# A queue order in a two-layer kernel: ScalarE takes one group's transposed input out of PSUM ahead of the other group's second square

## The reference

```
h = layernorm(x) * (1 + ca) + sa ;  x = x + ga * attention(h)
h = layernorm(x) * (1 + cb) + sb ;  x = x + gb * ffn(h)

fp4_linear(x, w) = fp4_quant_dequant(x) @ fp4_quant_dequant(w).T     # blocks of 16
ffn(h) = fp4_linear(silu(fp4_linear(h, w_gate)) * fp4_linear(h, w_up), w_down)   # 128 -> 352 -> 128
```

## Time and profile before

| | us |
|---|---|
| median of 3 runs | 1372.24 |
| lowest, highest | 1369.85, 1372.98 |
| the profiled execution's own time | 1373.02 |
| its span in the profile | 1371.2 |
| busy in the span: PE, DVE, POOL, ACT | 1128.8, 1057.5, 930.0, 625.6 |
| TensorE's mean granted clock | 0.899 of full speed |

### The profile page before, as it was taken

How to read it: one execution, slowest core, us unless ns; L and a number is a source line. 1 busy time by engine, 2 the same in 40 slices (tenths; PEclk the granted TensorE clock), 3 DMA queues, 4 the chain that set the end, 5 groups by cost and what they waited for, 6 DMA issues and landing times. The chain is left out here.

```text
span 1371.2 us, 29825 instructions
## 1 busy us (share of the span) xinstructions
PE 1128.8 (82%) x10832; PEld 711.5 (52%) x10832; DVE 1057.5 (77%) x1468; ACT 625.6 (46%) x1217; POOL 930.0 (68%) x808
## 2 busy tenths in 40 slices
PE   5889999989999989999999996586657776856865
PEld 2245565645655645655655655354335554545654
DVE  4588968868878768779789776677797777789895
ACT  2245645536546446455456452345444343423332
POOL 3379878768788768798798773333578686684331
PEclk9699999999999989999999997688868886887988
DMA  5112112112111111121121120000000000000000
GB/s 151 35 36 59 37 32 60 41 27 56 41 44 41 37 40 47 36 54 43 28 56 43 31 57 21 8 1 1 0 0 0 1 1 1 0 8 9 9 16 23
DMA packets 48627, 42.17 MB, mean 31 GB/s; under 512 B 7869, under 2 KB 46808, under 8 KB 48472
## 3 DMA queue, kind: packets, MB, share of 16 engines
q1 hardware_dynamic: 48040, 39.36, 11.6%
q10 hardware_dynamic: 432, 0.79, 0.2%
HBM read 6.42 MB, written 2.10 MB: 6 GB/s over the span
## 5 line engine op out<-in xcount | busy, mean ns | idle before, releaser
L509 ACT ACTIVATE a_probs<-a_ps_s 128x512 f32<-128x512 f32 x512 | 303.8, 596 | 326.6 <-PE a_ps_s L417 322.4
L742 POOL TENSOR_TENSOR a_p_lo<-a_probs 128x512 f16<-128x512 f32 x384 | 419.0, 1113 | 34.2 <-ACT a_probs L509 31.8
L670 DVE TENSOR_REDUCE a_nmx<-a_ps_m 128x2 f32<-128x1024 f32 x256 | 311.4, 1217 | 34.6 <-PE a_ps_m L400 33.9
L433 PE MATMUL a_ps_o<-a_v_hi,a_probs 128*128 128x65 f16 x2048 | 244.1, 196 | 15.4 <-DVE a_p_lo L677 7.9
L434 PE MATMUL a_ps_o<-a_v_lo,a_probs 128*128 128x64 f16 x2048 | 241.4, 194 | 0.0
L435 PE MATMUL a_ps_o<-a_v_hi,a_p_lo 128*128 128x65 f16 x2048 | 241.1, 195 | 0.0
L433 PEld LDWEIGHTS a_ps_o<-a_v_hi,a_probs 128*128 128x128 bf16 x2048 | 189.9, 99 | 87.9 <-issue 58.9
L415 PE MATMUL a_ps_s<-a_qq,a_kk 128*128 128x512 f16 x512 | 198.0, 387 | 8.2 <-issue 5.3
L434 PEld LDWEIGHTS a_ps_o<-a_v_lo,a_probs 128*128 128x128 bf16 x2048 | 191.8, 99 | 25.1 <-issue 1.5
L417 PE MATMUL a_ps_s<-a_qq,a_k_l 65*128 65x512 f16 x512 | 198.3, 387 | 0.0
L435 PEld LDWEIGHTS a_ps_o<-a_v_hi,a_p_lo 128*128 128x128 f16 x2048 | 191.5, 98 | 0.0
(11 more groups left out here) (234 smaller groups left out, 2108.7 us busy)
## 6 DMA issues: line engine op xcount, KB each, us to landing
a_qq<-a_rhi SPq DMA_DIRECT2D x128, 128.0 KB, 2.4
a_qq<-a_rlo SPq DMA_DIRECT2D x128, 64.0 KB, 2.1
a_kk<-a_rhi SPq DMA_DIRECT2D x64, 64.0 KB, 2.0
a_k_l<-a_rlo SPq DMA_DIRECT2D x32, 64.0 KB, 2.1
out_x<-x_sb SPq DMA_DIRECT2D x8, 256.0 KB, 2.3
a_qq<-a_nmT SPq DMA_DIRECT2D x64, 2.0 KB
a_probs<-in_wq ACTq DMA_DIRECT2D x1, 512.0 KB, 5.1
a_wo<-in_wo SPq DMA_DIRECT2D x1, 512.0 KB, 12.3
```

The costliest lines, as they stand in the source:

```text
L433: nc.tensor.matmul(out, hi, v_hi[:, b % 2, kt, g, 0:65], start=(kt == 0), stop=False)
L509: nc.scalar.activation(probs[:, p % 2, kt, h, :], ps_s[:, i % 2, :], ACT.Exp, scale=DH0 ** -0.5).then_inc(exp_done, 1)
L670: nc.vector.tensor_reduce(nmx[:, p % 2, i:2 * QT:QT], ps_m[:, n % 2, :, :], axis=X, op=ALU.max, negate=True).then_inc(free[n % 2], 1)
L742: nc.gpsimd.tensor_tensor(p_lo[:, p % 2, kt, h, :], pr, pr.bitcast(BF16)[:, 1:2 * L:2], ALU.subtract).then_inc(lo_pool, 1)
```

## The change

T1 moves from the third `place_group` call to the second, where it stands between S2 and C2. In the shared ticks, the list before reads C2, KVG (or LY, PS), T1; the list after reads T1, C2, KVG (or LY, PS). The order changes for ScalarE and TensorE. In the ticks with KVG, T1 also has an earlier place in the ring, so the KVG of the tick change banks. No instruction, size or wait is added or taken away.

```diff
     each(place_group, ("GH0", "HS", "GU1", "GH1", "C1", "N1"))
     each(place_round, ("SM", "SR", "RES", "ON", "DEN"))
-    each(place_group, ("S2", "C2"))
+    each(place_group, ("S2", "T1", "C2"))
     each(place_round, ("LHT", "KVG", "OT", "LY", "PS", "LX"))
-    each(place_group, ("TD", "T1"))
+    each(place_group, ("TD",))
     each(place_round, ("PP", "SP", "GATE", "SIG"))
```

## The result

The changed kernel takes 1377.71 us (median of 18 executions, 1374.0 to 1386.46) against 1371.09 for the kernel before (18 executions, 1369.02 to 1375.45): a ratio of 1.0055 with a 95% interval of [1.004, 1.0071], so it is slower by 7.5 us (0.0055 of 1371; the interval is 5.5 to 9.7; the two medians are 6.6 us apart). The forecast was 1370.8 us with a range up to 1375.4.

A forecast was written before the change was run, and what follows sets the result against it. It took the second part to be bound by a chain passing from engine to engine, DVE not full. Its per-group terms summed to 1.4 us gained from the 1372.24 us median: 1370.8 us, range 1366.8 to 1375.4.

The forecast's parts named there:

- rival C: The change doesn't do what it says: GU has no slack to give, signs cancel; 0, time 1372.2 us; chance 0.13.
- T1 of 1: Group 1's T1: GU starts earlier, but HS ends with GpSimd's product; +0.5 us gained, bounds 0 and 2.3.
- Groups 8, 10 and 12: T1's transposes move into TensorE's pause before LY, shortening the path by their own slot; +1.65 us gained in sum.
- T1 of 4: Group 4's T1 trades places with KVG on TensorE, so GU starts after four KVG; -0.3 us, a loss.
- 13: Group 13's T1: C2 about 1 us later but just hidden, GU 0.9 earlier, HS ends with GpSimd's product; 0.
- 7: Group 7's T1: GpSimd is the bound, its product starts without idle time; 0.
- T1 of 6: Group 6's T1 trades places with KVG on a cold clock, GU comes later; -0.9 us, bounds 0 and -2.4.
- Rival A: Two-input instructions' windows decide: HS gets in before GpSimd's next product; gain 4 us, time 1368.2; chance 0.25.
- T1 of 14 and 15: Last ticks: T1's copy is late, so C2 comes 0.69 us later and DVE's N2 with it; -0.7 and -1.3 us.
- rival B: Slower: ScalarE's queue holds the square behind a copy that isn't ready; +3.2 us, time 1375.4; chance 0.17.
- T1 of 9: Group 9's T1: its transposes no longer stand between C2 and the following KVG; +0.9 us gained, bounds 0 and 1.1.
- T1 of 2 and 3: TensorE's bank wait goes for group 2 (+0.85 us); DVE's waits for two Silu go for group 3 (+0.7 net).

The follow-up runs named there:

- e2: T1 moved ahead of C2 only for groups 4, 6 and 9, all else the kernel before: 1378.68 us, ratio 1.0042.
- x1: The changed kernel, but in groups 13 to 15 ScalarE does C2 before T1's copy, as in the kernel before: 1374.49 us, ratio 1.002.
- e1: T1 moved ahead of C2 only for groups 13, 14 and 15, all else the kernel before: 1379.29 us, ratio 1.0044.
- w6: The changed kernel plus extra identity products in the tail, none ahead of GU: 1377.37 us, ratio 1.003 against the kernel before.
- a1: The changed kernel plus one extra DVE memset at the start of the second part: 1377.76 us, ratio 1.0038 against the kernel before.
- a2: The changed kernel plus three extra DVE memsets at the start of the second part: 1385.45 us, ratio 1.0092 against the kernel before.
- w3: The kernel before with T1 early for groups 13 to 15 and extra identity products, none ahead of GU: 1373.76 us, ratio 1.001.
- e6: For groups 13 to 15 T1 placed behind C2, which gives the kernel before's instruction lists, so a repeat of it: 1373.87 us, ratio 1.0006.
- w1: The kernel before plus extra identity products from group 12 on, also ahead of GU: 1378.85 us, ratio 1.0041.
- w5: Extra identity products, none ahead of GU, T1 of groups 13 to 15 behind C2; otherwise the kernel before: 1376.27 us, ratio 1.0026.
- c1: The kernel before plus one DVE memset of 0.48 us at the start of the second part: 1376.18 us, ratio 1.0019.
- w4: The kernel before plus extra identity products in the tail, none ahead of GU: 1377.71 us, ratio 1.0033.

## Why the prediction was wrong

What was right. The change does what it says (rival C falls). T1 of 1 brings 0.64 (forecast 0.5; its own two times, 891.9 and 892.56, differ by 0.66), for the reason given: HS now runs beside GpSimd's product and ends with it. By the rule of the Trainium skill that the prediction cited (page "SBUF — State Buffer", section "Who interferes with whom") the two exclude each other, and the trace agrees once more: 2.63 us beside it, 0.83 clear of it. Groups 8, 10 and 12 bring 0.6, 0.7 and 0.4, together 1.7 (forecast 1.65). T1 of 4 costs 0.6 (forecast 0.3), of 13 nothing in itself; 7 brings 0.6 where I had 0. T1 of 6 costs 1.0 in the trace of the change (forecast 0.9), but 3.7 in that of e2 with the same order there, so this agreement is luck. Rival A's first window opened: HS at 1224.59, which the prediction calls group 12's and which is group 11's, takes 1.14 us instead of the 2.50 of the earlier trace rows. DVE keeps this only until 1232, where L1324, which also reads two SBUF tensors, takes 2.31 us beside GpSimd's product instead of 0.69; none of A's 2.6 us came.

The steps that failed:

- **T1 of 14 and 15: -0.7 and -1.3.** This was the mechanism of rival B, which got only 0.17. The queue's own cost was right: 2.0 forecast, 2.2 measured as waits of DVE for C2. Its size on the path was not: 5.5 us in the trace, 5.4 against x1's and 4.8 in time. The term was mis-sized because it priced only the wait. Of TensorE's work behind the waits, the down products twice and the second half of GU met a lower clock, and that costs 3.2 us more. My upper bound of 2.8, two whole squares, was no bound, since it had no term for the products behind them.
- **T1 of 9: +0.9.** It is -1.0 to -1.3. The KVG products and the PS behind them took the durations of the low clock throughout (the last two KVG 2.14 each and PS 3.66, where before the last KVG's large product took 1.52 and PS 2.05), and DVE's wait for Silu rose from 1.80 to 3.09 us at 1180. The order was as foreseen, and the durations were carried over from a trace in which the clock had risen at 1176.6 us instead of 1178.3, 3.4 us earlier as counted from the start of the second part. In e2's trace, where PS ran at the high clock, the same order gained 0.5.
- **T1 of 2 and 3: +0.85 and +0.7.** Both are about 0. In the tick of 2, TensorE's wait of 0.85 did go and GU starts 0.7 us earlier, but DVE's lead behind it is 0.7 us as well: the 0.64 that group 1 had gained, and no second gain. DVE, which had come to N2 earlier by those 0.64, spends them on a longer wait for C2 (2.34 us instead of 1.51). The prediction added the two gains. In the tick of 3 the wait for C2 rises by 1.3 (1.52 to 2.81), against 1.2 that the waits for Silu give back; GU there starts 1.3 us earlier and then runs at the low clock (4.87 us for eight products).

The sum of these: tail 3.5, T1 of 9 2.0, T1 of 2 and 3 1.5, together 7.0, against the 6.9 between a forecast gain of 1.4 and a traced loss of 5.5. What the first two have in common is that durations from the trace before were moved along with their products, as if TensorE's clock moved along too. One reading of the prediction doesn't matter for its sum: it says that the copy for T1 of 15 starts when it does today (1340.80), while its 1342.22 takes it to start right behind the transposes, as it then did.

What the runs show and what they don't. Shown: the exchange on ScalarE in the last three ticks costs about 5 us, from both sides (e1 against before, the change against x1); by the traces the clock makes over half of it; with T1 ahead of KVG the exchange has the other sign, in two of the three ticks with a wait for the PSUM bank. Not settled: how the remaining 2.7 us are made up. The pieces don't add (20.5 against 7.5), a shift of half a microsecond alone costs 2.6, and which untouched ticks lose differs from run to run. One execution of a list can also differ from another: at 1034 us the traces of w6, a1 and a2 lose 3.0 to 3.4 us more than those of the change and of x1, with the same order there. The remaining 2.7 may be of this kind; no run shows it. It stays open whether T1's earlier place in the early and middle ticks is bad by itself or for where it puts the later products. No version beat the kernel before; the best one with T1 early is w3 at +1.4, whose interval includes no difference, and it needs extra products that cost something themselves.

## What to carry to other kernels

In a chain over several engines with the tensor engine often idle, its clock is a part of the schedule: a wait of w ahead of a burst of products costs w plus what the burst loses if the clock falls in the pause, here 0.7 becoming 5.4 us in two runs, and a range for a reordering needs that term for gains and for losses. Before moving a copy ahead of other work in an in-order queue, ask for each place separately whether its input is ready by then (if not, what is behind it waits) and whether it frees a buffer that another engine waits for (if so, it has to go first). Copy first was better by 9.4 us in the three KVG ticks and worse by 5 in the last three. And gains along a chain don't add when the second only lets the first one through. Where effects are under 0.5%, run a pure shift and an equal program beside the experiment, since otherwise the phase passes for a cause.

## What the runs showed of the hardware

- The same sixteen GU products take 5.3 us or 7.9 us, by when they start; a KVG product 1.17 or 2.14; sixteen PS rows 1.95 or 3.62 to 3.66.
- The granted clock's low stretches come back at the same places of a schedule. Eight traces have the same list up to group 12 (before, e1, e6, w1 to w5); from 200 to 420 us into the second part, their low stretches begin within about 1 us of each other. But a small change moves them: with the schedule half a microsecond off (c1), the low clock came at 1278.0 us, inside a pause of 3.21 us, where the kernel before, with a pause of 2.75, had stayed high from 1268.8 to 1302.9. And the changed order has two outcomes: from about 171 us into the second part the clock is low for 6.8 us in the traces of the change and of x1, and for 13.7 in those of w6 and a1.
- Extra products in TensorE's pauses raised the clock and still lost. Six of them ahead of GU delayed it. Twelve ahead of the down products took 2.84 us at the high clock, longer than the pause, and DVE waited 1.44 us behind them. From 1300 us to the end the clock averaged 0.92 (w4) instead of 0.83 on the order before, which became 4.5 us slower.
